# An expert layer: results stored by block number and gathered per tile, in place of scatters by token

## The reference, cut to what matters

```
x = x + attn(layernorm(x));  xf = layernorm(x)          # 4096 tokens x 128
gates = softmax(xf @ router_w)                          # 14 experts
top_v, top_i = top_k(gates, 2);  masked = top_v / (sum(top_v) + EPS)
routed = sum over the token's 2 experts e of masked[e] * (silu(rms(xf, rms_w[e]) @ w1[e]) @ w2[e])
shared = the same, ungated, for 2 further experts       # 128 -> 256 -> 128
out = x + routed + shared
```

## Time and profile before

| | |
|---|---|
| median of 3 runs | 324.9 us (323.02 to 326.68) |
| the profiled execution | 325.44 us, of which 323.7 us are the span of its instructions |
| busy in the span | PE 259.8, DVE 223.0, POOL 176.1, ACT 167.5 us |
| mean granted TensorE clock | 0.919 |

### The profile page before, as it was taken

How to read it: one execution, slowest core, us unless ns; L and a number is a source line. 1 busy time by engine, 2 the same in 40 slices (tenths; PEclk the granted TensorE clock), 3 DMA queues, 4 the chain that set the end, 5 groups by cost and what they waited for, 6 DMA issues and landing times.

```text
span 323.7 us, 9066 instructions
## 1 busy us (share of the span) xinstructions
PE 259.8 (80%) x2812; PEld 237.0 (73%) x2812; DVE 223.0 (69%) x842; ACT 167.5 (52%) x326; POOL 176.1 (54%) x234
## 2 busy tenths in 40 slices
PE   1894466783698769999998798889999999999930
PEld 0893464672586457889877687779989998999930
DVE  6999999679942388677778754334565766876682
ACT  1567436369677385666876463334434443444410
POOL 2589300000066004777777777577767777777770
PEclk9999585589799995999999979999999999999995
DMA  5892009679992000111111135332434475556372
GB/s 134 204 400 106 0 21 265 172 192 305 318 305 70 0 0 27 50 53 49 59 50 50 60 101 136 102 91 84 116 92 104 151 208 160 152 166 191 88 182 81
DMA packets 54742, 41.24 MB, mean 127 GB/s; under 512 B 6151, under 2 KB 50076, under 8 KB 54192
## 3 DMA queue, kind: packets, MB, share of 16 engines
q1 hardware_dynamic: 47712, 31.15, 34.4%
q0 software_dynamic: 4544, 8.44, 7.8%
q10 hardware_dynamic: 2448, 1.20, 1.5%
HBM read 28.70 MB, written 12.98 MB: 129 GB/s over the span
## 4 chain that ended last, share of the span: by engine, by line
PE 51%; DVE 16%; DMA 9%; ACT 8%; SPq 7%; issue 6%; DVEq 1%; ACTq 0%; POOLq 0%
PE bank L1632 8%; PE bank L1643 8%; PE bank L1548 4%; PE bank L1535 3%; PE bank L1611 3%; DVE u L756 3%; PE bank L1604 2%; PE bank L1437 2%; PE bank L1483 2%; PE bank L1509 2%; PE bank L1623 2%; DMA area<-kp_dram 2%; PE bank L1475 2%; DVE stats L711 2%; PE bank L1476 2%
## 5 line engine op out<-in xcount | busy, mean ns | idle before, releaser
L650 POOL DMA_INDIRECT y_dram<-u x78 | 78.7, 1009 | 29.4 <-issue 21.7
L640 POOL DMA_INDIRECT xs_dram<-area x64 | 63.1, 986 | 40.0 <-issue 38.5
L1008 DVE COPY v<-v 128x512 f32 x84 | 35.8, 432 | 21.6 <-issue 21.0
L1632 PE MATMUL bank<-xn,v 128*128 128x128 f32 x320 | 42.6, 276 | 0.0
L1643 PE MATMUL bank<-v,xn 128*128 128x128 f32 x312 | 41.2, 275 | 0.0
L1632 PEld LDWEIGHTS bank<-xn,v 128*128 128x128 f32 x320 | 38.9, 192 | 0.4
L1643 PEld LDWEIGHTS bank<-v,xn 128*128 128x128 f32 x312 | 38.0, 192 | 0.0
L1304 ACT ACTIVATE xn<-bank 128x512 f32<-128x512 f32 x40 | 23.9, 597 | 18.5 <-PE bank L1632 18.5
L1299 ACT COPY xn<-bank 128x256 f32<-128x256 f32 x41 | 15.2, 371 | 30.5 <-PE bank L1623 27.7
L1025 DVE COPY u<-area 128x2 uint32<-128x2 uint32 x39 | 8.4, 216 | 24.6 <-PE bank L1643 24.6
L614 POOL TENSOR_TENSOR x_sb<-x_sb,outb_bc 128x1024 f32<-128x1024 f32 x4 | 9.4, 2382 | 20.7 <-DVE x_sb L832 20.7
(11 more groups left out here) (297 smaller groups left out, 618.9 us busy)
## 6 DMA issues: line engine op xcount, KB each, us to landing
area<-kp_dram SPq DMA_DIRECT2D x12, 512.0 KB, 6.6
area<-xs_dram SPq DMA_DIRECT2D x78, 64.5 KB, 1.8
area<-y_dram SPq DMA_DIRECT2D x8, 512.0 KB, 3.9
x_sb<-in_L_attn_x SPq DMA_DIRECT2D x4, 512.0 KB, 7.8
area<-ab_dram SPq DMA_DIRECT2D x2, 1024.0 KB, 6.2
xn<-ab_dram SPq DMA_DIRECT2D x2, 1024.0 KB, 10.8
xn<-kp_dram SPq DMA_DIRECT2D x4, 512.0 KB, 6.5
out_x<-x_sb SPq DMA_DIRECT2D x8, 256.0 KB
```

The costliest lines, as they stand in the source:

```text
L640: pool.indirect_dma_start(out=xs_dram.ap(), out_offset=bass.IndirectOffsetOnAxis(ap=pos[:, k, i:i + 1], axis=0), in_=hx[:, i, k, :], in_of ...
L650: pool.indirect_dma_start(out=y_dram.ap(), out_offset=bass.IndirectOffsetOnAxis(ap=ybi[:, z:z + 1].bitcast(U32), axis=0), in_=yb[:, z, :], ...
L1008: v.tensor_copy(wc[:, z % STEP], v1_flat.rearrange("p (w m) -> p w m", w=2)[:, :, bass.ds(r, HID)]).then_inc(wc_ready, 1)
L1632: last = mm(bank[2 + p % 2][:, HID * j + P * c:HID * j + P * c + P], wc[:, (2 * p + j) % STEP, 1, P * c:P * c + P], xsT[:, p % 3, P * j:P ...
```

## The change

- SP stores the results of a pair, two blocks, to `y_dram` by block number (`store_pair`, 39 stores). The semaphores `y_out` count them in rounds of three pairs, and DVE holds pair q until the store of pair q - 3 has landed. Ahead of that SP fills `y_dram` (5.1 MB) with zeros, behind the weights.
- DVE works out for each route the row in which its result lies (`block_steps`, and in pairs 1 to 6 three wide operations for each k; `finish_slots`). The route number leaves `hx`, `xs` and `xinit`, whose rows shrink from 129 to 128 words, and with it the second copy in `hx` and DVE's copy of the numbers.
- GpSimd waits, chunk by chunk, until the rounds that hold the chunk's blocks have landed, and gathers its 8 x 128 rows with 8 indirect DMAs straight to `yl` (64 in all, line 651 of the changed kernel). The number of rounds is read from `ltab`; by the counts above it is 3, 5, 5, 7, 8, 10, 11 and 12, so the chunks wait for pairs 8, 14, 14, 20, 23, 29, 32 and 35.
- The loop holds 6 units of the shared experts instead of 12, one every six pairs; the last 6 follow the loop on TensorE and ACT, and DVE adds them between the last chunks.
- All nine pads of SP are written ahead of its first load (ACT writes five), and the checks of the numbers that SP reads are left out.

```diff
-    SH_FIRST, SH_FILL, SH_LOOP = 18, 2, 2
+    SH_FIRST, SH_FILL, SH_LOOP, SH_TAIL = 18, 2, 1, 6
...
+            y_blocks = y_dram.ap().rearrange("(b p) c -> p b c", p=P)
+            sp.dma_start(y_blocks, xinit[:].unsqueeze(1).broadcast_to([P, NBLK, D])).then_inc(y_zero, 16)
...
+            def store_pair(q):
+                z = 2 * q % UNROLL
+                sp.wait_ge(yb_ready, 2 * q + 2 + 2)
+                sp.dma_start(y_blocks[:, 2 * q:2 * q + 2], yb[:, z:z + 2]).then_inc(y_out[q % ROUND], 16)
...
-                if t_ == 4:
-                    write_pads(PADS_FIRST, SP_PADS - PADS_FIRST)
...
+            for q in range(PAIRS):
+                store_pair(q)
+                t_ = UNROLL + 2 * (q - 1)
+                if q % 2 and t_ < NBLK:
+                    load_rows(t_, min(4, NBLK - t_))
...
+                if stored < CH and q >= PAIRS_TO[stored] + 8:
                     store(stored)
...
-            for z in range(STEP):
-                pool.wait_ge(yb_ready, z + 1 + 2)
-                send_block(z)
-            with pool.Fori(0, LOOPS) as it:
-                for z in range(UNROLL):
-                    pool.wait_ge(yb_ready, it * UNROLL + (STEP + z + 1 + 2))
+            pool.wait_ge(slot_ready, 1)
+            for c in range(CH):
+                for z in range(ROUND):
+                    pool.wait_ge(y_out[z], landed[c])
                     g_.sem_inc(pool_turn, 1)
-                    send_block((STEP + z) % UNROLL)
+                for k in range(2):
+                    for i in range(TILES * c, TILES * c + TILES):
+                        pool.indirect_dma_start(out=yl[:, k, i, :], out_offset=None, in_=y_dram.ap(),
+                                                in_offset=bass.IndirectOffsetOnAxis(ap=slot_of[:, k, i:i + 1], axis=0),
+                                                bounds_check=NBLK * P - 1, oob_is_err=False).then_inc(results_in[c], 16)
...
+            def pass_bounds(k):
+                v.drain()
+                v.tensor_tensor(passed, pos[:, k].rearrange("p (c i) -> p c i", c=CH).unsqueeze(3)
+                                .broadcast_to([P, CH, TILES, 2 * E]), tiles_by(bounds), ALU.is_ge)
+
+            def weigh_bounds():
+                v.drain()
+                v.tensor_tensor(passed, passed, tiles_by(shifts), ALU.mult)
+
+            def sum_bounds(k):
+                v.drain()
+                v.tensor_reduce(moved[:, k].rearrange("p (c i) -> p c i", c=CH), passed, AX.X, ALU.add)
...
                 if k == 0:
-                    dve.wait_ge(results_in[c], 16)
+                    dve.wait_ge(results_in[c], 16 * 2 * TILES)
...
-                if q >= STEP:
-                    dve.wait_ge(yb_out[q % STEP], 32 * (q // STEP))
+                if q >= ROUND:
+                    dve.wait_ge(y_out[q % ROUND], 16 * (q // ROUND))
                 finish_pair(q, q % STEP)
+                if q == 0:
+                    block_steps()
+                if q == 1 or q == 4:
+                    pass_bounds(q // 4)
+                if q == 2 or q == 5:
+                    weigh_bounds()
+                if q == 3 or q == 6:
+                    sum_bounds(q // 6)
+                if q == 6:
+                    finish_slots()
...
-                act.wait_ge(h0_ready, c + 1)
-                a.copy(hx[:, k, 1, 0:D], hx[:, k, 0, 0:D]).then_inc(hx_ready, 1)
```

More of the change, by code:

```diff
@@ L359, in build_kernel @@
         yb_ready = sem("yb_ready")
-        yb_out = [sem(f"yb_out{z}") for z in range(STEP)]
+        y_out = [sem(f"y_out{z}") for z in range(ROUND)]
+        y_zero = sem("y_zero")
+        slot_ready = sem("slot_ready")
         results_in = [sem(f"results_in{c}") for c in range(CH)]
@@ L441, in _ @@
                 sp.dma_start(w2_sb[:, E:EA, c], w2s.rearrange("e (c p) d -> c p e d", c=HC)[c]).then_inc(ew2_in, 16)
+            y_blocks = y_dram.ap().rearrange("(b p) c -> p b c", p=P)
+            sp.dma_start(y_blocks, xinit[:].unsqueeze(1).broadcast_to([P, NBLK, D])).then_inc(y_zero, 16)
             sp.nop().then_inc(all_in, 1)
             sp.wait_ge(ptab_ready, 1)
[L445 to L451, removed]
+            _, ends = nc.values_load_multi_w_load_instructions(
+                ptab[0:1, 0:SP_PADS], engines=[mybir.EngineType.SP], min_val=0, max_val=(NULL - 1) * P,
+                skip_runtime_bounds_check_because="a count of routes added to a region's start lies in the region")
+            for r in ends:
+                sp.dma_start(xs_dram.ap()[bass.ds(r, P), :], xinit[:]).then_inc(pads_out, 16)
             sp.wait_ge(btab_ready, 1)
@@ L457, in load_rows @@
                 _, places = nc.values_load_multi_w_load_instructions(
-                    btab[0:1, first:first + n], engines=[mybir.EngineType.SP], min_val=0, max_val=NULL)
+                    btab[0:1, first:first + n], engines=[mybir.EngineType.SP], min_val=0, max_val=NULL,
+                    skip_runtime_bounds_check_because="VectorE bounds every entry by the number of the spare block")
                 if first < EARLY:
@@ L488, in _ @@
                 load_rows(t_)
-                if t_ == 4:
-                    write_pads(PADS_FIRST, SP_PADS - PADS_FIRST)
[L492 to L503, removed]
+            sp.wait_ge(y_zero, 16)
+            stored = 0
+            for q in range(PAIRS):
[3 more added lines that the diff above has]
+                    load_rows(t_, min(4, NBLK - t_))
+                if q == PAIRS - 4:
+                    for z in range(STEP, STEP + 4):
+                        sp.wait_ge(xs_in[z], 16 * LOOPS)
+                        sp.nop().then_inc(xs_in[z], 16)
+                if stored < CH and q >= PAIRS_TO[stored] + 8:
                     store(stored)
                     stored += 1
[L506 to L515, removed]
             for c in range(stored, CH):
@@ L1022, in finish_pair, with finish_slots @@
+            def sum_bounds(k):
+                v.drain()
+                v.tensor_reduce(moved[:, k].rearrange("p (c i) -> p c i", c=CH), passed, AX.X, ALU.add)
+            def finish_slots():
+                v.drain()
+                v.scalar_tensor_tensor(out=slot_of, in0=moved, scalar=float(P), in1=pos, op0=ALU.mult,
+                                       op1=ALU.add).then_inc(slot_ready, 1)
             def finish_pair(q, p):
-                row = z = 2 * p % UNROLL
+                z = 2 * p % UNROLL
@@ L1066, in _ @@
                     summed += 1
-            dve.wait_ge(so_added, NT)
-            for n in range(summed, 2 * CH):
+            for n in range(summed, 2 * (CH - 2)):
+                add_results(n // 2, n % 2)
+            add_tail(SH_LAST, 4)
+            for n in range(2 * (CH - 2), 2 * (CH - 1)):
+                add_results(n // 2, n % 2)
+            add_tail(SH_LAST + 4, SH_TAIL - 4)
+            for n in range(2 * (CH - 1), 2 * CH):
                 add_results(n // 2, n % 2)
```

166 lines of the change are left out of this document (106 added, 60 removed).

## The result

The changed kernel takes 327.0 us (median of 20 runs, 324.2 to 331.8) against 325.2 us for the kernel before, run beside it: ratio 1.0062, 95% interval 1.0036 to 1.0089. It is slower, by 0.6% where 1.7% was forecast. The profiled execution took 328.76 us (span 327.0) and so lies 1.8 above its median; the one of before lies 0.3 above. Times are medians of all runs, while ratios leave out runs that a slower state of the chip lengthened, so a ratio can differ by some tenths of a per cent from that of two medians.

The account below looks back on a forecast made before the run. TensorE bounds the loop, GpSimd is as full. Chunk 1's gathers start at 248.3, the 56th at 319.3; landing 321.9, additions 324.3, end 329.4; with 1.74 and 0.2% off, 330.5 against 324.9, 1.7% slower (327.5 to 335, chance 0.57).

Parts of the forecast that it names:

- The mechanism: From pair 14's landing on, GpSimd falls behind and 56 gathers in a row set the end.
- the store and the end 5.1: End of the kernel, behind the last additions: the store and the end take 5.1 us, from 324.3 to 329.4.
- the landing of pair 14's store: Ahead of chunk 1's gathers: issued at 243.8, landing takes 4.2 us (bounds 1.8 and 5.5), so 248.0.
- The pitch: GpSimd's gathers from chunk 1 on: 1.29 us each, so 55 steps take 71.0 us.
- Rival 3: Gathers on GpSimd are dearer: 1.40 us each gives 336.7, 1.62 gives 349; chance 0.18.
- rival 1: Gathers are cheap, from 1.0 us down, and the loop sets the end: 317 to 320, 2% faster; chance 0.12.
- The work added to DVE is hidden behind nothing: Pairs 0 to 11: DVE's added work moves pair 11's copy to 236.2; without it TensorE would be there at 232.4.
- continuously busy up to pair 10: Sign of being right: DVE continuously busy from pair 0 to about pair 10, its copies later than TensorE.
- Rival 2: DVE's added work fits into TensorE's waits; pair 14 is 3.8 us earlier: 326.7, no difference; chance 0.13.
- ScalarE's copy: Ahead of pair 0: dropping ACT's second copy, 0.53 us standing three times in the chain, gains 1.0 of 1.6 us.
- SyncE's relief: SP's start: pads move ahead and checks shrink, removing TensorE's waits for rows at pairs 4 and 6; no separate gain.
- What was taken at nothing: Later gates (13 us of cover), tail units (10.7 us on TensorE) and zeros (36 us of writing) cost nothing.

Follow-up runs that it names:

- The first two experiments: Changed kernel with 24 gate numbers in place of 8: 323.2 us, ratio 0.9947; changed kernel without the second expert's 32 gathers: 316.4 us, ratio 0.974.
- ScalarE's copy back: Changed kernel with ScalarE's second copy of the normalised rows restored and read by the second expert's scatters: 328.8 us, ratio 1.0065.

## Why the prediction was wrong in size

The mechanism held: a gap between chunks 0 and 1 and none behind it, VectorE waiting for gathers (10.7 us, 7.7 of them ahead of the last additions), GpSimd's row setting the end. The first two experiments showed it by moving the row and by halving it. The sum came out 2.4 us too high for the profiled execution, and that execution lies above its median. By the prediction's terms:

```
term                                     forecast   profiled execution
pair 0's copy                             203.3      202.1
pair 0's copy to pair 14's                 38.9       41.2  (39.1 to 39.6 in four others)
pair 14's copy to chunk 1's first gather    6.1        3.1  (3.1 to 4.0)
55 gathers, start to start                 71.0       72.9
landing and additions                       5.0        5.0
last addition to the end                    5.1        2.9
span                                      329.4      327.0
```

Two steps failed, and together they made the sum 5.2 us too high.

**The first is "the store and the end 5.1".** It read the 5.1 behind the last addition as the store's, and carried it over. In the kernel before it is GpSimd's drain behind 78 scatters, the last six of spare blocks; SyncE was through 2.3 us earlier. Adding and taking away such transfers moved the end. In the changed kernel drain and store end within 0.1 us of each other, so nothing of the 2.3 was left to carry over. That also means that the chain shown at the end, through DMA and additions, has a second one beside it that the views do not show.

**The second is the landing of pair 14's store, which was mis-sized.** 4.2 was taken from the 128 KB stores to `kp_dram`. In the changed kernel's trace pair 14's store was issued 0.46 us after its copy's start, where 1.6 was forecast for the loads ahead of it, and landed 1.83 later; chunk 1's first gather started 0.83 behind that, where 0.3 was taken. The Trainium skill ("DMA: Bandwidth & Descriptors", Anatomy of one DMA) gives 2.0 us and bytes / 436e3, so 2.3 for 128 KB, for DMAs that GpSimd issues; this store is SyncE's. By it the sum would have been 1.9 lower, and the 1.8 to 1.9 measured lies nearer to it than to 4.2: the row of another tensor was the worse guide.

**The pitch erred to the other side**, and gave 1.9 us back: 1.32 in the mean, not 1.29. Most steps are 1.30; up to 310 us one to three in eight are 1.33 to 1.52, and of the last seven none. What stretches them was not tried. Rival 3's 1.40 did not come, nor rival 1's 1.0.

**"The work added to DVE is hidden behind nothing" is wrong**, though pair 11 came 32.8 us behind pair 0, as the sum had it (32.9). That the sum met this number is luck. Half of the wide operations taken away left pair 14 where it was, and VectorE waited for TensorE 0.97 us at pair 3 and 1.01 at pair 11, so it was not continuously busy up to pair 10, which the prediction had named as a sign of being right. TensorE's waits of over 0.3 us from pair 0's copy to pair 11's in the changed kernel:

```profile
209.93 1.16 PE L1669 MATMUL bank<-v,area 128*128 128x128 f32 x8 [1.29 <-DVE x_sb L938]
...
223.67 0.41 PE L1681 MATMUL bank<-ident,area 128*128 128x128 f32 x2 [0.64 <-DMA area<-xs_dram]
...
226.73 1.15 PE L1690 MATMUL bank<-xn,v 128*128 128x128 f32 x8 [0.51 <-DVE v L1005]
```

Two of them are for VectorE: 1.29 for the addition of a shared unit, which stood behind the first wide operation, and 0.51 for a fetch. With the 0.64 for rows they are 2.4 of the 32.8 us, which leaves some 30.4 for TensorE's own work (an estimate), where the prediction summed 29.1. Rival 2, that the work finds room, was right in the main and wrong in its price of 3.8: pair 11 came 32.2 behind pair 0 with half of the work. Its 326.7 lies next to the measured 327.0 by luck.

**ScalarE's copy** at 1.0 agrees with the last normalisation, but a gain at pair 0's copy is not shown. What does show there is about 1 us of another part: from the table of experts to pair 0's copy it is 12.5 to 13.3 us in five traces of the kernel before and its variants, 11.3 to 11.6 in nine with the changed start, and 12.2 in the one with SyncE's old start, so that start seems to be most of it. **SyncE's relief** "is in the sum already", and was, but for the 0.64 above: the loop was summed without waits for rows. Undone, it costs 4.6 us, more than any other part that was undone.

**What was taken at nothing** (later gates, tail units, zeros) was nothing: chunk 7 did not wait, though pairs 14 to 35 came at 2.5 us and not at 2.3; the tail units ended at 312.8; the zeros took 19 us and not 36, landing at 116 ahead of the first scatter, and a second writing was free.

**From the profiled execution to the median.** TensorE waits 1.89 us at a place where it does not in four other traces of kernels with the same loop, and pair 14 is that much later:

```profile
240.75 0.41 PE L1681 MATMUL bank<-ident,area 128*128 128x128 f32 x2 [1.89 <-issue]
```

That is as much as the 1.8 by which this execution lies above the median. With 39.3 for that term the sum of the measured ones is 325.1, and with 1.7 for what lies around the span 326.8, next to the median of 327.0. It is not shown to be the cause, since the first scatter's start alone differs by 3.5 us between executions.

## What to carry to other kernels

Before a stretch at the end is carried over to another kernel, ask which engine's program ends last: the chain shows the last work, not the last program. A queue that issues at a fixed pace (here GpSimd at 1.3 us for 128 rows) is judged from the moment at which its input opens, since idle time ahead of that cannot be used later; so the gate ahead of the long row is the place to gain, and a few small operations that sharpen it turned a loss of 0.6% into a gain of 0.5%. A transfer's time is best taken from a row of the same kind in both ends, and where there is none, the bounds matter more than the nearest size.

## What the runs showed of the hardware

GpSimd's closing drain ended 6.62 us behind the last of 128 indirect DMAs in all eight traces with that number, and 7.76 behind the last of 142 in all three. Where transfers were only added to a kernel it grew by about 0.08 us each: to 6.94 with 132 and to 8.25 with 148. Where some were taken away it did not shrink below that of their kernel: 7.92 with 96 (128 before) and 7.99 with 136 (142 before). So the number does not set it alone, and what does stays open.

At TensorE's 1.89 us wait a packet of an instruction queue moves; the DMA part of the changed kernel from 238 to 241 us (packets, MB, share):

```profile
q8 instruction: 1, 0.02, 2.0%
```

In the other trace with such a wait (ScalarE's copy back: 2.1 us, pair 14 at 42.3 behind pair 0) such a packet comes at the same place, 37 us behind pair 0's copy; in five traces with pair 14 at 39.1 to 39.8 the last one comes at 19 to 23. The Trainium skill ("Runtime: NRT & Kernel Launch", Instruction fetch mechanics) says that engines load code in blocks of 16 KiB and that a taken branch to a block not at hand has to wait for it. The packet's size, 16 KB, agrees. The place agrees only roughly, since the wait ends 0.5 us ahead of the branch that closes the loop's second turn, and no run here separates it from chance.
